# A two-layer graph network on one core: the adjacency's low halves from GpSimd to VectorE, two T steps from Z to U

## What is computed

```python
h = relu(layernorm(x))
Xw = h @ Wv + bv;  sj = Xw @ aw[:d, 0];  si = Xw @ aw[d:, 0]
T = adj * exp(leaky_relu(sj[None, :] + si[:, None] + ab, 0.2));  T /= T.sum(-1)
H = h @ Wk[0] + (T @ h) @ Wk[1] + (T @ T @ h) @ Wk[2] + sum(bk)
x = x + relu(H)
h = relu(layernorm(x))
Ah = adj + I;  dh = rsqrt(Ah.sum(-1))
x = x + relu(dh[:, None] * (Ah @ (dh[:, None] * (h @ kernel))) + bias)
```

## Time and profile before

| | before |
|---|---|
| median of three runs | 863.5 us |
| the profiled execution | 863.14 us |
| its span on the core | 861.3 us |
| TensorE busy | 787.2 us (91%) |
| VectorE busy | 641.9 us (75%) |
| ScalarE busy | 509.6 us (59%) |
| GpSimd busy | 300.1 us (35%) |

### The profile page before, as it was taken

One profiled execution on the slowest core, in us unless ns is written; L12 is line 12 of the kernel. 1 busy time (PEld: TensorE's weight loads), 2 busy tenths in 40 slices (PEclk: granted clock), 3 DMA queues, 4 the chain that ended last, 5 costly groups with the idle time before them and its releaser, 6 DMA issues.

```text
span 861.3 us, 15910 instructions
## 1 busy us (share of the span) xinstructions
PE 787.2 (91%) x6092; PEld 755.9 (88%) x6092; DVE 641.9 (75%) x1407; ACT 509.6 (59%) x997; POOL 300.1 (35%) x247
## 2 busy tenths in 40 slices
PE   2957999899999999899998999989999999989998
PEld 2747899899989999898998989989998999989998
DVE  4557597876978678885879759787687867887565
ACT  1497555766467664675647745576646766468232
POOL 1003134433254331632326314443225333163416
PEclk9978999999999999999999999999999999999999
DMA  5446341871437533575317734187143861356512
GB/s 183 147 122 202 129 135 46 251 243 62 136 104 243 193 99 99 168 248 169 108 50 226 252 117 135 39 258 242 62 135 104 243 204 39 98 163 213 179 34 99
DMA packets 65227, 128.70 MB, mean 149 GB/s; under 512 B 6272, under 2 KB 32256, under 8 KB 65152
## 3 DMA queue, kind: packets, MB, share of 16 engines
q1 hardware_dynamic: 55936, 94.13, 33.3%
q10 hardware_dynamic: 9216, 33.56, 13.3%
HBM read 119.28 MB, written 8.39 MB: 148 GB/s over the span
## 4 chain that ended last, share of the span: by engine, by line
PE 71%; DVE 16%; ACT 5%; issue 4%; POOL 2%; DMA 1%; ACTq 0%; DVEq 0%
PE acc L907 17%; PE acc L909 16%; PE acc L908 16%; PE da L818 13%; PE db L818 5%; PE tp L810 3%; DVE a_raw L658 3%; DVE tg_e L615 3%; ACT t_hi L401 2%; DVE t_lo L619 2%; DVE z_tmp L670 1%; POOL a_lo L309 1%; DVE o_tile L675 1%; DVE ht_lo L586 1%; ACT tg_e L391 1%
## 5 line engine op out<-in xcount | busy, mean ns | idle before, releaser
L907 PE MATMUL acc<-g_hi,t_hi 128*128 128x256 f32 (+1 forms) x1024 | 294.2, 287 | 15.7 <-issue 8.2
L909 PE MATMUL acc<-g_hi,t_lo 128*128 128x256 f32 (+1 forms) x1024 | 290.8, 284 | 0.0
L908 PE MATMUL acc<-g_lo,t_hi 128*128 128x256 f32 x1024 | 289.6, 283 | 0.0
L309 POOL TENSOR_TENSOR a_lo<-a_raw,a_hi 128x512 fp32r<-128x512 f32 x128 | 186.4, 1473 | 177.0 <-ACT a_hi L442 175.4
L907 PEld LDWEIGHTS acc<-g_hi,t_hi 128*128 128x128 f32 x1024 | 194.9, 190 | 16.3 <-issue 8.7
L908 PEld LDWEIGHTS acc<-g_lo,t_hi 128*128 128x128 f32 x1024 | 195.3, 191 | 0.0
L909 PEld LDWEIGHTS acc<-g_hi,t_lo 128*128 128x128 f32 x1024 | 195.1, 191 | 0.0
L907 PE MATMUL acc<-g_hi,a_hi 128*128 128x256 f32 x512 | 147.6, 288 | 25.4 <-POOL a_lo L309 25.3
L908 PE MATMUL acc<-g_lo,a_hi 128*128 128x256 f32 x512 | 144.2, 282 | 0.0
L909 PE MATMUL acc<-g_hi,a_lo 128*128 128x256 f32 x512 | 144.1, 282 | 0.0
L391 ACT ACTIVATE tg_e<-si,sij 128x256 f32<-128x256 f32 x256 | 110.0, 500 | 25.9 <-DVE t_lo L619 25.9
(11 more groups left out here) (86 smaller groups left out, 1458.7 us busy)
## 6 DMA issues: line engine op xcount, KB each, us to landing
tg_a<-adj_t_dram ACTq DMA_DIRECT2D x64, 512.0 KB, 4.0
a_raw<-adj_dram SPq DMA_DIRECT2D x64, 512.0 KB, 4.0
a_raw<-adj_t_dram SPq DMA_DIRECT2D x64, 512.0 KB, 5.2
h<-x_dram SPq DMA_DIRECT2D x8, 1024.0 KB, 5.5
x_res<-x_dram SPq DMA_DIRECT2D x64, 128.0 KB, 3.6
out_dram<-o_tile SPq DMA_DIRECT2D x64, 128.0 KB, 3.3
p<-wk_dram SPq DMA_DIRECT2D x1, 768.0 KB, 7.4
p<-bk_dram SPq DMA_DIRECT2D x1, 384.0 KB, 7.3
```

The lines of the kernel that those rows point to most:

```text
L309: nc.gpsimd.tensor_tensor(a_half(a_lo, i, h), a_raw[:, i % RS, h * N // 2:(h + 1) * N // 2], a_half(a_hi, i, h).bitcast(F32), ALU.subtract ...
L907: nc.tensor.matmul(acc[:, s, 0:n], l_hi, r_hi, start=(jt == 0), stop=False)
L908: nc.tensor.matmul(acc[:, s, 0:D], l_hi, r_lo, start=False, stop=False)
L909: ins = nc.tensor.matmul(acc[:, s, 0:n], l_lo, r_hi, start=False, stop=(jt == NT - 1))
```

## The change

All 128 subtractions for a_lo go from GpSimd's queue to VectorE's (a_low). The half steps 13 and 14 of T, (6, 1) and (7, 0), go from the end of Z to U chunks 0 and 1; the four that were in U follow one or two chunks later, two of them together after chunk 3, and Z chunks 2 and 4 have none. Row sums move by up to one chunk, the last two to after U chunk 6. The diagonals of blocks 6 and 7 move from after Z chunks 3 and 4 to after 2 and 3. The option to place t_lo on GpSimd, which was empty, is taken out.

```diff
-    T_Z = {i: HALVES[7 + i:8 + i] for i in range(8)}
-    T_U = {i: HALVES[15 + i:16 + i] for i in range(3)}
-    BEFORE_U = 15
-
-    ROWS_U = {0: (0,), 1: (1,), 2: (2,), 3: (3, 4), 4: (5, 6), 5: (7,)}
+    T_Z = {0: HALVES[7:8], 1: HALVES[8:9], 3: HALVES[9:10], 5: HALVES[10:11], 6: HALVES[11:12], 7: HALVES[12:13]}
+    T_U = {0: HALVES[13:14], 1: HALVES[14:15], 2: HALVES[15:16], 3: HALVES[16:18]}
+    BEFORE_U = 13
+
+    ROWS_U = {0: (0,), 1: (1,), 2: (2,), 4: (3, 4), 5: (5,), 6: (6, 7)}
...
-    DIAG_Z = {0: 4, 1: 5, 3: 6, 4: 7}
+    DIAG_Z = {0: 4, 1: 5, 2: 6, 3: 7}
...
-            def a_split(b, i, h):
-
-                pool.wait_ge(a_hi_done[h], b * NT + i + 1)
-                nc.gpsimd.tensor_tensor(a_half(a_lo, i, h), a_raw[:, i % RS, h * N // 2:(h + 1) * N // 2],
-                                        a_half(a_hi, i, h).bitcast(F32), ALU.subtract).then_inc(a_ready[h], 1)
...
+                for g in range(NG):
+                    power(rstd1, ve1, ve1_ready, b * NG + g + 1, rstd1_ready, slice(2 * g, 2 * g + 2))
...
-                    if not last:
+                    if not last and i in T_Z:
                         (step,) = T_Z[i]
                         t_step(b + 1, *step, False, between=next_half)
...
+            def a_low(b, i, h):
+
+                dve.wait_ge(a_hi_done[h], b * NT + i + 1)
+                nc.vector.tensor_tensor(a_half(a_lo, i, h), a_raw[:, i % RS, h * N // 2:(h + 1) * N // 2],
+                                        a_half(a_hi, i, h).bitcast(F32), ALU.subtract).then_inc(a_ready[h], 1)
...
+                a_low(b, 0, 0)
+                a_low(b, 0, 1)
                 for i in range(NT):
...
                     v_chunk(b, par, i)
+                    if i == 1:
+                        a_low(b, 1, 0)
+                        a_low(b, 1, 1)
...
+                a_low(b, 2, 0)
+                a_low(b, 3, 0)
                 for i in range(NT):
+                    if i > 1 and i in A_FIRST:
+                        a_low(b, *A_FIRST[i])
                     z_chunk(b, par, i)
+                    if i <= 1:
+                        a_low(b, *A_FIRST[i])
                     if i in DIAG_Z:
                         diag(b, DIAG_Z[i])
+                    if i in A_THEN:
+                        a_low(b, *A_THEN[i])
                     if not last:
-                        for step in T_Z[i]:
+                        for step in T_Z.get(i, ()):
                             t_step(b + 1, *step)
```

More of the change, by code:

```diff
@@ L33, in gnn_two_layers @@
     T_V = {-1: HALVES[2:3], 1: HALVES[3:4], 2: HALVES[4:5], 3: HALVES[5:6], 4: HALVES[6:7]}
-    T_Z = {i: HALVES[7 + i:8 + i] for i in range(8)}
-    T_U = {i: HALVES[15 + i:16 + i] for i in range(3)}
-    BEFORE_U = 15
-    ROWS_U = {0: (0,), 1: (1,), 2: (2,), 3: (3, 4), 4: (5, 6), 5: (7,)}
+    T_Z = {0: HALVES[7:8], 1: HALVES[8:9], 3: HALVES[9:10], 5: HALVES[10:11], 6: HALVES[11:12], 7: HALVES[12:13]}
+    T_U = {0: HALVES[13:14], 1: HALVES[14:15], 2: HALVES[15:16], 3: HALVES[16:18]}
+    BEFORE_U = 13
+    ROWS_U = {0: (0,), 1: (1,), 2: (2,), 4: (3, 4), 5: (5,), 6: (6, 7)}
     STATS_V = {0: (0, 1)}
     STATS_U = {0: (2, 3), 1: (4,), 2: (5, 6), 3: (7,)}
-    DIAG_Z = {0: 4, 1: 5, 3: 6, 4: 7}
+    DIAG_Z = {0: 4, 1: 5, 2: 6, 3: 7}
     A_FIRST = {i: (i + 2, 1) for i in (0, 2, 3, 4, 5)} | {1: (4, 0)}
     A_THEN = {0: (3, 1)} | {i: (i + 3, 0) for i in (2, 3, 4)}
-    LOW_ON_POOL = ()
     TS, RS = 2, 4
@@ L320, in batch @@
                     g1_split(b, i)
-                    for k, half in T_U.get(i, ()):
-                        if half == 1 and k - 1 in LOW_ON_POOL:
-                            t_low(b, k - 1)
                     if i == 3 and not last:
@@ L326, in batch @@
                 power(dh, row_a1, rows1_done, b + 1, dh_ready)
[L327 to L344, removed]
+                for g in range(NG):
+                    power(rstd1, ve1, ve1_ready, b * NG + g + 1, rstd1_ready, slice(2 * g, 2 * g + 2))
             power(rstd0, ve0, ve0_ready, 1, rstd0_ready)
-            for k, half in HALVES[:BEFORE_U]:
-                if half == 1 and k - 1 in LOW_ON_POOL:
-                    t_low(0, k - 1)
             for b in range(0, B - 3, 2):
@@ L615, in t_step @@
                     nc.vector.tensor_tensor(tg_e[:, s], tg_a[:, s], tg_e[:, s], ALU.mult).then_inc(prod_ready, 1)
-                if half == 1 and k > 0 and u not in LOW_ON_POOL:
+                if half == 1 and k > 0:
                     dve.wait_ge(t_hi_done, b * NU + u + 1)
```

## The result

The changed kernel takes 886.98 us (median of 4 runs, 885.57 to 887.85) against 863.27 us before: 1.0272 times as long, 95% interval 1.0258 to 1.0287, or 23.7 us more. Its profiled execution has a span of 885.9 us, 24.6 us above the 861.3 us of the one shown of before.

What follows compares the result with a forecast made beforehand. TensorE, busy 91% of the span, was taken to bound the kernel. Profiled 863.1 us plus 1.9 (setup) plus 6 x 2.9 (batches) less 1.4 (last batch) gave 881.0 us; 8-in-10 range 856 to 889.

Steps and rivals of the forecast that it cites:

- The walk through the queues: Z to L0 of one middle batch, instruction by instruction: Z gains 2.4 us, U loses it, L0 starts 2.9 us later.
- VectorE's load: Whole run: 88 us of low halves come, 93 us go at most, so VectorE's total stays near 642 us.
- The low halves: VectorE in each Z stage: 12 x 0.60 = 7.2 us come, 8.9 us of waits behind GpSimd go.
- The row sums: ScalarE before L0: the last two, between g1_hi 6 and ht_hi 0, cost about 1.0 us even with VectorE on time.
- A (faster): Whole kernel: VectorE is relieved and reaches U early, each batch gains 3.1 us, 842 us in all; chance 0.19.
- B (wash): Z: both raw blocks arrive in time, VectorE is 2.85 us earlier, 861 to 863 us in all; chance 0.09.
- Rival D: TensorE: new gaps drop its clock to 1.2 GHz, one chunk per batch takes double, +17 us, 898 in all; chance 0.03.
- setup: Before the first L0: T subtraction 7 comes later and row sums precede ht_hi 0, so L0 starts 1.9 us later.
- Six batches: Middle batches, L0 to L0: each takes 2.9 us longer, period 105.2 instead of 102.3 us.
- the last transition: U of the last batch: chunk 6 waits until about 386.6, so 1.4 us of Z's gain stays.
- the later raw loads: SP's queue: raw loads 0 to 3 follow up to 4 us later, are wanted in L0, and cost nothing.
- Two waits in the middle batch: VectorE in Z: diagonals 6 and 7, moved up, wait 1.3 and 1.55 us for their raw blocks to land.

## Why the prediction was right, and where it was short

**Direction and mechanism: right.** The walk through the queues gave, on the scale of the rows, U chunk 6 at 387.95 and L0 at 397.5; the trace has 388.02 and 397.59. T subtractions 5, 6 and 7 were put at 374.6, 381.7 and 386.6 and stand at 374.79, 381.83 and 386.74. TensorE's waits in that batch were said to be under 1 us before Z chunks 5 and 6, 2.4 before U chunk 6 and 1.6 before L0; they are 1.46 (chunk 6), 1.95 and 1.12. VectorE's load was said to stay near 642 us and is 631.8: 94 us went for the 84 that came, where 93 had been called the most. The low half was taken at 0.69 us and is 0.684.

**The low halves: right as a term, and tested.** The forecast let 7.2 us of them come against 8.9 us of waits per Z stage, 1.7 us to the good. Alone they give about 11 us over the run, 1.6 us from L0 to L0.

**The row sums: right.** "About 1.0 us" even with VectorE on time was measured at 9.1 us over the seven starts of L0, 1.3 us each.

**Rivals.** A (faster) and B (wash) failed in the changed kernel, but B named the right lever: with both blocks in time the run took 862.8 us, where B said 861 to 863. What it takes is only another place for two transfers in SP's queue. Rival D, the lower clock, came in part, and is not what made the kernel slower: the kernel before with new T steps and row sums takes 884.42 us with a full granted clock (1.00) from 94 to 880 us. See the last section.

**The size: 17.9 us forecast, 24.6 us in the profiled execution.** L0 starts, changed kernel and kernel before:

```profile
89.69 0.50 PE L802 MATMUL da<-wa_hi,ht_hi 128*128 128x512 f32 x1 [1.19 <-DVE ht_lo L551]
...
722.83 0.50 PE L802 MATMUL da<-wa_hi,ht_hi 128*128 128x512 f32 x1 [1.39 <-DVE ht_lo L551]
```

```profile
701.38 0.48 PE L818 MATMUL da<-wa_hi,ht_hi 128*128 128x512 f32 x1
```

With 87.40 from the earlier trace rows: setup 89.69 - 87.40 = 2.3 us (forecast 1.9). Six batches (722.83 - 89.69) - (701.38 - 87.40) = 19.2 us, 3.2 each (forecast 2.9). What follows, 163.1 against 159.9 us: **+3.1 us where the forecast had -1.4**. This is the term that was mis-sized, 4.5 of the 6.7 us. The step said that the last transition keeps 1.4 us of Z's gain, and that its last batch adds nothing. Both parts failed.

Up to U chunk 6 it took 97.7 us from the last L0, and 95.8 before: +1.9 instead of -1.4. The forecast took both blocks to land in 4.1 to 4.7 us. The load of block 7 in that batch, and what TensorE then did (the columns of the window: us, busy and count of PE, PEld, DVE, ACT, POOL, granted clock, DMA share, GB/s):

```profile
a_raw<-adj_t_dram SPq DMA_DIRECT2D x1, 512.0 KB, 6.4
```

```profile
794.87 0.55 PE L891 MATMUL acc<-g_hi,a_hi 128*128 128x256 f32 x1 [3.05 <-DVE a_lo L628]
```

```profile
794.00:800.40 6.40, 5.53 (x26) 5.57 (x27) 6.33 (x11) 2.85 (x6) 0.00 (x0) 0.50 0.31 92
```

The load took 6.4 us to landing, TensorE idled 3.05 us, and the granted clock, fallen to 0.50 already in the gap, stayed there to the end of the window: 26 matmuls every 0.213 us instead of 0.119, another 2.4 us for TensorE. Not all of that is in the run's time. T unit 7 and U chunk 6 then stand so:

```profile
819.23 1.23 DVE L584 TENSOR_TENSOR t_lo<-tg_e,t_hi 128x1024 fp32r<-128x1024 f32 x1 [1.12 <-ACT t_hi L366]
```

```profile
820.51 0.39 PE L891 MATMUL acc<-g_hi,t_hi 128*128 128x258 f32 x1
```

T unit 7 is ready at 820.46 and chunk 6 starts at 820.51, so a TensorE at full clock would have waited here for VectorE. VectorE itself had waited 0.51, 0.79 and 0.30 us for TensorE's chunks on the way, so of the 2.4 us the clock can have cost 1.6 at most (an estimate; no run separates them). The bounds for the landing had been taken from two transfers of one batch; the median over all 64 loads of the line, 5.2 us, stood on the page of the profile of before and was not used.

From U chunk 6 to the end it took 65.44 us, and 64.18 before: 1.3 us where the forecast had nothing. It had put the later raw loads at nothing because they "are wanted in L0". The last batch's V follows U with no L0 between. There VectorE waits 4.6 us for the first blocks instead of 1.6, among them

```profile
832.70 0.29 DVE L623 TENSOR_TENSOR a_raw<-a_raw,ident 128x128 f32<-128x128 f32 x1 [1.86 <-DMA a_raw<-adj_t_dram]
```

and TensorE waits for VectorE behind it. With the row sums back (and all else as in the changed kernel) this stretch is 64.3 us.

**Two waits in the middle batch** were forecast at 1.3 and 1.55 us and were 0.65 and 2.19: off singly, right in sum (2.85 and 2.84). Both loads were issued when the forecast said (353.41 and 356.80 on its scale); block 6 landed after 3.5 us instead of 4.1, block 7 after 4.7 instead of 4.55. In the other five batches of the middle the two waits sum to 2.8 to 3.1 us. That 4.1 and 4.55 hit the sum is partly luck, as the 6.4 us of the last one shows.

**Two side remarks of the prediction.** The Trainium skill, DMA: Bandwidth & Descriptors, "Anatomy of one DMA", gives its fit for transfers that GpSimd issues; these are issued by SP, and took 3.5 to 6.4 us where it gives 3.2. The 0.2 us that the prediction worked out from it for the second wait would be 1.1 us by its own walk, since the first wait would be 0.9 us shorter. And the stalls of Z were put at 4.1 us a batch, 28.7 in all: the terms beside it give 4.2, of which 3.6 us (25.3 in all) are idle time of TensorE. Neither is in the forecast's sum.

## What to carry to other kernels

When a step is moved up in an in-order queue, look up when its input lands, and which queue issues that load behind what: here two loads one store earlier were worth 24 us, and the same edit was worth nothing before the step had moved. Work that goes from a slow helper engine to the busy one can be free, if the helper was blocking it; price it by the busy engine's instructions with and without the other beside them. Take a landing time from the spread over the run, not from one batch, where the engine behind it has no slack. And walk the last batch by itself: a stage that hides a delay in the others may be missing there.

## What the runs showed that was not expected

The granted clock fell behind a gap of 1.95 us. Before U chunk 6 of the batch shown TensorE had waited so long for t_lo, and the stretch behind it reads:

```profile
397.00:400.20 3.20, 3.20 (x20) 3.20 (x20) 2.83 (x16) 1.64 (x4) 2.35 (x2) 0.64 0.14 58
```

On average 0.64, with matmuls every 0.215 us for 2.4 us, the 1.2 GHz level. Behind a gap of 2.09 us in the kernel before it had stayed at full speed (granted 1.00 from 345 to 375 us). The Trainium skill, TensorE: Matmul & The Clock Gate, "HAM oscillation", warns of such falls where idle gaps repeat, in an example with longer gaps. The traces agree that they happen, and show that the length of the gap does not decide alone. In the changed kernel the clock fell behind three of six gaps of 1.94 to 1.96 us before U chunk 6. In the kernel before with the loads ahead it fell behind three of seven gaps of 1.99 to 2.11 us in Z, and the time was the same (863.12 us). In U of the changed kernel the fall cost nothing either: from L0 to L0 the three batches with it take 105.6, 105.4 and 105.4 us, the three without it 105.5, 105.6 and 105.7. At the start of L0 TensorE waits for ht_lo in all six, and the fall disappears in that wait.

The Trainium skill, SBUF — State Buffer, "SBUF: two separate sides", says that a VectorE instruction with two SBUF inputs and a GpSimd instruction that reads SBUF hold a shared port pair in turn, as an exclusive lock and "not a bandwidth split". The traces agree in both directions: with GpSimd's subtractions gone the diagonal went from 1.38 to 0.29 us, and z_tmp, which reads PSUM and one tensor in SBUF, had been 0.47 to 0.49 us in all 64 cases, beside GpSimd or not. VectorE's own trace does not show these waits as idle time: they are in the length of the instruction, which is why its busy time fell when work was added.
